# A two-layer kernel on one core: TensorE's program for the loops of layer 2 written out turn by turn

## The reference, cut to what matters

```
xn = layernorm(x)
s  = linear attention(xn)                  # 16 heads of 64, feature map elu + 1
g  = silu(attention of 16 heads of 8 + mixture of 8 experts, top 2 (xn))
x  = x + s * g                             # layer 1
xn = layernorm(x)
s  = gated linear attention(xn)            # 16 heads of 64, chunks of 64 tokens, then a gelu FFN
g  = silu(mixture of 8 experts, top 1 (xn))
x  = x + s * g                             # layer 2
```

## The kernel before, in words

| lines | what |
|---|---|
| 1084, 1088 | decay between the tokens of a chunk, from `at3` (VectorE, lines 1780 and 1782), after a mask that needs its PSUM bank free; the bank before it is read by the key copies of line 1791 and the record of line 2141 |
| 1097 | decay to the end of a chunk |
| 777, 799, 808 | a step of the expert tiles (`tile_step`): transpose, first product, second product; steps 0 to 7 are spread over the turn, and with six tiles the last two end it |
| 1109 to 1139 | norms (1109; VectorE reads them at line 2047), values (1115), their scaling (777, 1127), keys turned (777), gate (1139) |
| 1153 | scores, 64x64 matmuls |
| 1168 | running sums of the gates, 64x64 |
| 1185 | states of the chunks, 64x64 |
| 1200, 1213 | outputs from within the chunk and from the state, 64x64 |
| 777, 816 to 848 | inputs and gates of the next sequence (stage P), the rank for the routing |
| 1224, 1074, 1238, 1074, 1247 | output product, next queries, FFN, next keys, second FFN product |

## Time and profile before

### The profile page before, as it was taken

One profiled execution on the slowest core, in us unless ns is written; L12 is line 12 of the kernel. 1 busy time (PEld: TensorE's weight loads), 2 busy tenths in 40 slices (PEclk: granted clock), 3 DMA queues, 4 the chain that ended last, 5 costly groups with the idle time before them and its releaser, 6 DMA issues.

```text
span 2145.7 us, 61336 instructions
## 1 busy us (share of the span) xinstructions
PE 1774.0 (83%) x23060; PEld 1275.5 (59%) x23060; DVE 1277.2 (60%) x3518; ACT 998.2 (47%) x2242; POOL 216.0 (10%) x235
## 2 busy tenths in 40 slices
PE   6999999987988889857888788887888888888652
PEld 4566566665665656635575556565666666766552
DVE  5676666675566566545465657575666566665312
ACT  2454444444454455434554455355544445555332
POOL 0000010000000000020110011001111100110122
PEclk9999999999999999979999999999999999999887
DMA  3222222221112211221212221120121111121473
GB/s 134 82 91 91 97 97 100 108 81 62 55 61 71 71 48 43 91 83 51 71 47 65 61 70 47 59 58 27 58 63 57 48 57 54 51 62 37 164 214 115
DMA packets 97603, 161.01 MB, mean 75 GB/s; under 512 B 14729, under 2 KB 66057, under 8 KB 94090
## 3 DMA queue, kind: packets, MB, share of 16 engines
q1 hardware_dynamic: 88170, 135.05, 19.2%
q0 software_dynamic: 9248, 23.17, 3.5%
HBM read 96.45 MB, written 61.69 MB: 74 GB/s over the span
## 4 chain that ended last, share of the span: by engine, by line
PE 58%; DVE 13%; issue 11%; ACT 9%; SPq 3%; DMA 2%; another core or an unknown queue 2%; POOL 1%; DVEq 0%; ACTq 0%; POOLq 0%
PE psum L920 5%; PE psum L799 3%; PE psum L777 3%; PE psum L990 3%; PE psum L1005 3%; PE psum L910 3%; PE psum L1224 3%; PE psum L1012 2%; PE psum L1115 2%; PE psum L808 2%; PE psum L1074 2%; PE psum L959 2%; PE psum L1088 2%; PE psum L1153 2%; PE psum L844 2%
## 5 line engine op out<-in xcount | busy, mean ns | idle before, releaser
L1454 ACT ACTIVATE pts<-psum 128x512 f32<-128x512 f32 x192 | 99.1, 603 | 173.9 <-PE psum L959 173.4
L1936 DVE TENSOR_REDUCE mneg<-psum 128x2 f32<-128x512 f32 (+1 forms) x192 | 119.1, 683 | 63.1 <-PE psum L939 35.2
L684 POOL DMA_INDIRECT rows<-h,recA x64 | 61.8, 965 | 871.7 <-DVE recA L1679 744.2
L799 PE MATMUL psum<-txT,wt 128*128 128x128 f32 x864 | 118.6, 281 | 2.4 <-ACT txT L1329 2.4
L808 PE MATMUL psum<-wt,tg 128*128 128x128 f32 x528 | 82.8, 289 | 43.2 <-DVE tg L1646 43.2
L920 PE MATMUL psum<-wa,xT_s 128*128 128x512 f32 x256 | 117.8, 604 | 0.0
L1074 PE MATMUL psum<-xT_s,wa 128*128 128x256 f32 x512 | 115.7, 379 | 0.0
L708 POOL DMA_INDIRECT rows<-xn,recC x32 | 33.4, 1043 | 804.5 <-DVE recC L2119 693.4
L799 PEld LDWEIGHTS psum<-txT,wt 128*128 128x128 f32 x864 | 108.4, 196 | 6.9 <-ACT txT L1329 4.1
L1074 PEld LDWEIGHTS psum<-xT_s,wa 128*128 128x128 f32 x512 | 96.1, 190 | 13.2 <-issue 0.8
L808 PEld LDWEIGHTS psum<-wt,tg 128*128 128x128 f32 x528 | 71.1, 200 | 47.2 <-DVE tg L1646 47.2
(11 more groups left out here) (276 smaller groups left out, 4330.4 us busy)
## 6 DMA issues: line engine op xcount, KB each, us to landing
wt<-in_wB SPq DMA_DIRECT2D x84, 384.0 KB, 3.0
outs<-pbd SPq DMA_DIRECT2D x16, 1024.0 KB, 7.0
wt<-in_wD SPq DMA_DIRECT2D x24, 578.0 KB, 3.4
wa<-in_wD SPq DMA_DIRECT2D x15, 578.0 KB, 3.6
tx<-rows SPq DMA_DIRECT2D x132, 64.0 KB, 3.1
outs<-ty SPq DMA_DIRECT2D x132, 64.0 KB, 1.6
rows<-pbd SPq DMA_DIRECT2D x64, 128.0 KB, 1.8
rows<-pbd SPq DMA_DIRECT2D x8, 1024.0 KB, 3.9
```

What stands on the lines that cost most here:

```text
L799: last = mm(bank(f"th{j}")[:, c * P:(c + 1) * P], view[s][:, c * P:(c + 1) * P], txT[:, s, :], start=True, stop=True)
L1454: af(pT[:, n, :], bank(f"e{n}"), ACT.Exp, scale=float(HD) ** -0.5).then_inc(*frees(f"e{n}"))
L1936: ins = v.tensor_reduce(mneg[:, int(n >= 4), col:col + hs], sc, AX.X, ALU.max, negate=True)
```

## The change

On TensorE alone, a segment with stage C is built turn by turn, with the turn a Python number. Segments 6 and 9 thereby stop being loops on TensorE: their bodies stand 6 and 7 times in its program, with constants in the waits. The matmuls, their order, their banks and the values that the waits come to are the same. The other four engines keep all their loops, TensorE those of segments 2 and 3.

```diff
@@ -1285,9 +1285,10 @@
                 if n == 1:
                     pe.wait_ge(sem("first_weights"), 16 * NFIRST[0])
                     pe.wait_ge(sem("zeros"), ZEROS)
-                if times == 1:
-                    segment(n, 0)
-                    body()
+                if times == 1 or "C" in stages:
+                    for i in range(times):
+                        segment(n, i)
+                        body()
                 else:
                     with pe.Fori(0, times) as i:
                         segment(n, i)
```

## The result

The changed kernel takes **2109.17 us**, the median of 14 runs (2098.03 to 2112.76), beside 2131.48 us for the kernel before, also of 14 runs (2116.07 to 2144.82). The ratio is 0.989, with a 95% interval of 0.986 to 0.992: 22.3 us or 1.1% faster. The direction is as forecast, the size is not: 37.3 us were forecast, and 2109 lies 9 us outside the range. The three runs shown ahead of the prediction (2120.31) were on the fast side of the fourteen. The changed kernel's profiled execution took 2111.97 us, its span is 2110.2 us. Lines of code behind the change are one higher than before (1084 and all of `attention1` keep their numbers, the loop's own line is now 1293).

A forecast was written before the change was run, and what follows sets the result against it. TensorE bounds the kernel, refetching layer 2's program every turn and waiting at branches. Segment 6's 33.6 us plus segment 9's 4.2 make 37.8, scaled 37.3 off 2120.31: 2083 us, range 2067 to 2100.

The forecast's parts named there:

- Segment 6, edges: Five branches between turns of segment 6: TensorE's idle time before the next turn's first matmul goes, 19.8 us.
- Start of a turn, segment 6: First matmul to line 1153: five turns no longer start at the lower clock after idle time, 2.9 us gained.
- Dense stretch, segment 6: Lines 1153 to 1213, small matmuls issued faster than fetched: 18.81 us a turn becomes 17.0, 10.9 us gained.
- The walk: Layer 2 written out: borders of fetched instruction blocks move from turn to turn, where a loop keeps them fixed.
- the block size: TensorE's instructions are fetched in blocks of 256; 252 matmuls and loads were seen between two holes.
- Dense stretch, segment 9: Lines 1153 to 1213 in seven turns: 0 change; ends 4.4 us gained and 13 lost, 6 as far as borders reach.
- Segment 9, edge and start: Six edges keep a wait for VectorE's key copy but give 2.6 us; one start at the lower clock gives 1.6.
- The rest of a turn: Waits worked out in registers get constants; register instructions run beside queued matmuls, so 0 gained.
- Rival (a): Segment 6 and 9 edges gain, but walking borders are no better than fixed: 26.6 us gained, 2094 us; chance 0.20.
- Rival (c): No gain: a layer 2 turn fits TensorE's instruction memory and its branch is cheap, 2118 us; chance 0.04.
- Pace: Rival in the experiments: straight code is fetched more slowly than a loop's, wherever block borders lie; no chance given.

The follow-up runs named there:

- second profiles: One more profiled run of each kernel: the kernel before, unchanged, measured 2154.12 us; the changed kernel, unchanged, measured 2131.2 us.
- Experiment 11: Kernel before with segment 6 a loop of three turns of two sequences each, so every second edge has no branch: 2155.36 us, ratio 1.002.
- Experiment 2: Kernel before with segment 9 alone written out, segment 6 still a loop: 2138.55 us, ratio 1.003.
- experiment 3: Kernel before, both loops kept, with 128 idle instructions early in TensorE's program, moving later borders half a block: 2146.77 us, ratio 1.008.
- experiment 4: Changed kernel with 35 idle instructions ending each turn of segment 9 and 170 early, so its borders stop walking: 2127.06 us, ratio 0.998.
- experiment 1: Kernel before with segment 6 alone written out, segment 9 still a loop: 2102.9 us, ratio 0.987.
- experiment 5: Kernel before, both loops kept, with 64 idle instructions ahead of segment 6 and 50 ahead of segment 8: 2141.29 us, ratio 0.994.
- experiment 8: Kernel before with segment 6 written out, segment 9 a loop, and 10 idle instructions ahead of segment 8: 2115.51 us, ratio 0.984.
- experiment 6: Kernel before with segment 6 written out, segment 9 a loop, and 40 idle instructions ahead of segment 8: 2135.36 us, ratio 0.993.
- experiment 10: Kernel before with segment 6 written out, segment 9 a loop, and 24 idle instructions ahead of segment 8: 2137.0 us, one run.
- experiment 9: The changed kernel run again, unchanged, on the second chip: 2131.2 us, ratio 0.990 to the kernel before.
- experiment 7: Kernel before with segment 6 written out, segment 9 a loop, 100 idle instructions early and 148 ahead of segment 8: 2177.09 us, one run.

## Why the prediction was right on the edges and wrong on the sum

Point by point, first profile against first profile, over segments 6 to 9 (976.2 us before, 961.9 after, 14.3 gained; 17.5 between the second profiles; the other 5 to 8 us of the 22.3 between the medians lie in stages whose code is the same, and I can't place them):

- **Segment 6, edges:** 19.8 forecast, 19.8 measured. The edge into segment 7, read from the trace of before, was the changed kernel's edge indeed. Experiment 11 gives the same price for an edge.
- **Start of a turn, segment 6:** 2.9 forecast, about 4.0 measured (5.1 by the windows, less 1.1 of missing records). The reason was only half right: four of the five turns without idle time at the edge still begin at a granted clock of 0.91 (19.7 us), and three of the five in the second profile.
- **Dense stretch, segment 6:** 10.9 forecast, **1.7 measured**. This is the first failed step. I took 17.0 us a turn; it was 18.5. The walk itself was right, and so was the block size; the turns differ (16.4 to 20.0 over the two profiles) by a little more than the 16 to 19 expected. What failed is the value of a place drawn anew: I had seen 16.18, 16.81, 18.66 and 18.81 and took 17.0, next to the lower two, which were measured at a granted clock of 1.00 throughout. Their mean was 17.6, and even that is below what came. Two things are in it. The idle time in the holes fell by 3.5 us in six turns (24.6 to 21.2), not by 10.9; and the busy time rose by 1.8 (88.19 to 89.97), with four of six turns partly at the lower clock, a cost that the term left at nothing.
- **Dense stretch, segment 9:** 0 forecast, with 6 us lost as "as far as a walking border reaches"; **12.1 lost** (and 19.2 between the second profiles). This is the second failed step, the same error with the sign of a loss: the bound took 18.66 as the worst place, and turns of 19 to 21.8 occur. Of the 12.1, 5.3 are holes and 6.9 busy time at the lower clock; the loop before had none of the latter. Experiment 2 shows the loss by itself, experiment 3 shows that a loop at a bad place loses as much (18 us), experiment 4 that straight code with a fixed place gets part of it back. That the holes bring the lower clock is argued from its fall behind them; no experiment changed the one without the other.
- **Segment 9, edge and start:** 2.6 + 1.6 forecast, together 3.5 measured (8.8 between the second profiles, where four starts before were at 0.91). VectorE is behind the branch as argued, by the 1.18 us that were read. The edge gave 3.6 (10.7 before, 7.1 after), as the sum took off 6 x 0.17 for the next bank, which isn't in the 10.7; the start gave nothing.
- **Segments 7 and 8:** left out as no change, 3.7 us lost (0.3 gained between the second profiles). Borders moved there too.
- **The rest of a turn:** 0 forecast; in segment 6 some 3.5 us went there, which none of the terms above holds.

The two dense terms are 10.9 - 1.7 + 12.1 = 21.3 us of the 23.5 between 37.8 forecast and 14.3 measured. The rest nearly cancels. Of the 26 us between the forecast time of 2083 and 2109, though, 11 are the time before, 2120.31 from three runs and 2131.48 from fourteen; 15 are the gain, 22.3 for 37.3. Rival (a), the edges alone, was the nearest, 26.6 us of gain, and it too took the loss in segment 9 for small. Rival (c) is refuted for this change: the branches cost what their rows say. (Segment 3 isn't wholly without fetches, as the prediction has it: its first turn shows 3 packets, the five behind it none.) But the idea in it, a turn that fits, came true where nobody had moved it on purpose (experiment 1), and then on purpose in experiments 5 and 8.

Pace, the rival in the experiments, is refuted: dense stretches of loops at bad places take 135.1 to 138.6 us in seven turns (experiments 3, 6, 10, 11), of the written-out segment 129.0 to 137.0 (experiments 2 and 9).

**Open:** what decides whether the loop of segment 9 is held. The traces record 1,789 instructions of TensorE in such a turn (experiment 5). Where it lies is my count from the holes seen. Ending 7 instructions into its eighth block it was held in four of six later turns (experiment 1); at about 17 in all six (5) or in four of six (8); at 31 and 47 in none (10, 6). Segment 6's loop, with 1,851, was fetched anew wherever it was kept. The Trainium skill ("Runtime: NRT & Kernel Launch", Instruction fetch mechanics) has TensorE hold 2048 instructions in blocks of 256; a turn within eight blocks would fit by that capacity. The runs agree at some of the places and contradict it at others: in experiments 6 and 10 the turn also lay within eight blocks, and every one was fetched anew. Its "mostly hidden" for crossing a border is not what dense code sees here: 15.4 us without borders (experiment 5), 16.2 to 20.0 with them at clock 1.00, and up to 21.8 with the lower clock.

## What to carry to other kernels

Code that is fetched while it runs has a cost that depends on where it lies, so any edit that changes the number of instructions moves that cost in all that follows; before an edit is judged, compare segments whose code did not change, and be ready to find its gain paid away there (experiment 11 gained 17 us and lost 16). A loop whose borders stand well is an asset: write out the loops that pay at the branch, and leave alone, or place, those that don't. When a term depends on a place that will be drawn anew, take the mean of all places seen, and let the range reach past the worst of them. Split a stretch into busy and idle time beside its granted clock before its length is put down to one cause. And where a wait changes its name, compare how many instructions each trace recorded.

## What the runs showed of the hardware that was not expected

- The same 593 matmuls took 16.2 to 20.0 us at a granted clock of 1.00 in the changed kernel's segment 9, by where the borders fell and by execution, and a stretch at the lower clock added 1.2 to 2.9 us of busy time; 21.8 us was the most in all. In two executions of the changed kernel the same turn of segment 9 differed by 0.1 to 2.3 us.
- A loop of 1,789 instructions can run with no fetch at all: the turn then takes 57.4 us instead of 59.8, the mean of segment 9 before (418.79 / 7), and its branch 0.21 us instead of 3.84. Fourteen instructions lay between four held turns (experiment 8) and none (experiment 10).
- A branch to code that isn't held is not of one size: 3.3 to 5.4 us, and up to 5.5 us of idle time where the loop begins just ahead of a border (experiment 7).
- Idle instructions on TensorE are not free: 128 of them delayed its first transposes from 16.1 to 26.5 us (experiment 3), about 80 ns each, and 35 at an edge cost some 1.7 us (experiment 4), about 50 ns each.
- Without any idle time at the edge of segment 6 the start of a turn was still at a granted clock of 0.91 in four of five turns. What was left ahead of it is a wait of 1.83 us for VectorE inside the last tile step, which stands ahead of the one turn at 1.00 as well; what sets the one from the other stays open.
